# Position attention in a decoder of twelve sublayers: the row maxima enter the score product as rows of the stacks

## The reference

```
qh = q.reshape(B, 8, dq, Lq)          # q = x: B 64, 64 rows, Lq 256
kh = k.reshape(B, 8, dq, Lk)          # k = v = context, dq = 8
qk = einsum('bhdq,bhdl->bhql', qh, kh) / sqrt(dq)
ret = einsum('bhql,bhdl->bhdq', softmax(qk), vh)
x = layernorm(x + gamma * ret)
```

## Time and profile before

| | |
|---|---|
| median of three runs | 5089.75 us |
| profiled execution | 5091.97 us, span 5090.2 us |
| busy over the span | TensorE 89%, VectorE 65%, ScalarE 40%, POOL 30% |
| mean granted clock of TensorE | 0.961 |
| the fifth stage | about 864.7 to 1546.7 us of the span |
| one tile in it | about 19.2 us |

### The profile page before, as it was taken

One profiled execution on the slowest core, in us unless ns is written; L12 is line 12 of the kernel. 1 busy time (PEld: TensorE's weight loads), 2 busy tenths in 40 slices (PEclk: granted clock), 3 DMA queues, 4 the chain that ended last, 5 costly groups with the idle time before them and its releaser, 6 DMA issues.

```text
span 5090.2 us, 89514 instructions
## 1 busy us (share of the span) xinstructions
PE 4538.3 (89%) x33622; PEld 3195.2 (63%) x33669; DVE 3297.4 (65%) x6372; ACT 2040.4 (40%) x4326; POOL 1518.0 (30%) x3018
## 2 busy tenths in 40 slices
PE   8988997899997988888379999999997999999788
PEld 6766886566665667776246666666664666666455
DVE  5657236677776757878755555555554666666798
ACT  4544113354553433333135445455542434334222
POOL 1111005333321223333234344334432322222122
PEclk9999998899998999999589999999998999999999
DMA  1012000333320000000100000000001000000000
GB/s 42 2 51 61 1 6 31 79 78 75 77 57 32 1 8 8 7 8 7 67 30 1 1 1 1 1 1 1 1 1 56 9 7 9 8 8 6 5 14 16
DMA packets 114779, 111.54 MB, mean 22 GB/s; under 512 B 20848, under 2 KB 107056, under 8 KB 109872
## 3 DMA queue, kind: packets, MB, share of 16 engines
q1 hardware_dynamic: 114352, 105.82, 8.0%
HBM read 89.00 MB, written 16.78 MB: 21 GB/s over the span
## 4 chain that ended last, share of the span: by engine, by line
PE 50%; DVE 19%; issue 15%; POOL 9%; DMA 4%; ACT 3%; SPq 2%; POOLq 0%; DVEq 0%; ACTq 0%
PE banks L2246 13%; PE banks L2489 4%; PE banks L727 4%; POOL factors L2696 3%; PE banks L1761 3%; DMA stack<-parts_x 3%; PE banks L2312 2%; PE banks L1172 2%; PE banks L754 2%; DVE neg_max L1085 1%; PE banks L1671 1%; PE banks L2410 1%; POOL rstd L265 1%; PE banks L2338 1%; PE banks L499 1%
## 5 line engine op out<-in xcount | busy, mean ns | idle before, releaser
L263 POOL TENSOR_TENSOR var_eps<-mean_var,ln_eps 128x1 f32<-128x1 f32 x384 | 83.1, 216 | 1635.5 <-DVE mean_var L259 1091.3
L1085 DVE TENSOR_REDUCE neg_max<-banks 128x2 f32<-128x512 f32 x512 | 343.4, 682 | 191.4 <-PE banks L1075 184.8
L1202 ACT ACTIVATE exps<-banks 128x512 f32<-128x512 f32 x512 | 304.7, 597 | 309.1 <-PE banks L1156 292.3
L2300 DVE TENSOR_TENSOR q_normed<-banks,factors 128x512 f32<-128x512 f32 x256 | 176.4, 689 | 230.5 <-POOL factors L2290 230.5
L2267 ACT ACTIVATE squares<-banks 128x512 f32<-128x512 f32 x256 | 153.1, 598 | 411.6 <-PE banks L2246 411.6
L2290 POOL TENSOR_TENSOR factors<-mean_squares,minus_half 128x4 f32<-128x4 f32 x256 | 258.0, 1008 | 21.6 <-POOL mean_squares L2286 0.5
L2672 ACT ACTIVATE squares<-q_normed 128x512 f32<-128x512 f32 x160 | 100.8, 630 | 396.0 <-DVE q_normed L2662 396.0
L1075 PE MATMUL banks<-stack,stack 128*128 128x256 bf16 x1024 | 202.6, 281 | 63.3 <-DMA stack<-parts_x 57.7
L1761 PEld LDWEIGHTS banks<-yT,w_swiglu 128*128 128x128 f32 x2048 | 238.5, 193 | 30.2 <-issue 29.9
L1761 PE MATMUL banks<-yT,w_swiglu 128*128 128x128 f32 x2048 | 247.4, 277 | 8.5 <-DVE hidden L1785 8.5
L1155 PE MATMUL banks<-stack,stack 128*128 128x256 bf16 x1024 | 253.1, 274 | 1.6 <-ACT exps L1202 1.2
(11 more groups left out here) (381 smaller groups left out, 11140.0 us busy)
## 6 DMA issues: line engine op xcount, KB each, us to landing
contextT<-in_ctxT SPq DMA_DIRECT2D x96, 128.0 KB, 2.5
parts_context<-parts SPq DMA_DIRECT2D x96, 64.0 KB, 2.0
parts_x<-parts SPq DMA_DIRECT2D x96, 64.0 KB, 2.0
stack<-parts_context SPq DMA_DIRECT2D x32, 192.0 KB
stack<-parts_x SPq DMA_DIRECT2D x32, 192.0 KB
x_all<-in_x SPq DMA_DIRECT2D x1, 4096.0 KB, 14.1
context<-in_ctx SPq DMA_DIRECT2D x64, 64.0 KB, 2.2
context<-in_ctx SPq DMA_DIRECT2D x32, 128.0 KB, 2.3
```

The source lines that it names most:

```text
L1085: v.tensor_reduce(self.mx[s][:, :, g:g + 1], self.bM[g % 2].rearrange("p (h c) -> p h c", h=DH), AX.X, ALU.max, negate=True).then_inc(self ...
L1202: self.nc.scalar.activation(self.e[n % 8][:], self.bE[n % 2].rearrange("p (l c) -> p l c", l=DH), ACT.Exp, scale=self.TOK ** -0.5).then_in ...
```

## The change

It does these things:

- The rows 96 to 127 of the context stacks are set to one at the start, in POOL's setup (four memsets of bf16).
- SP moves the three parts of the turned maxima from `neg_maxT` into rows 96, 97 and 98 of the query stack (`move_max_sp`, three DMAs a tile, 8 KB each). The score matmul runs over all 128 rows and so takes the maxima off itself; the selector, its load and its 32 matmuls a tile are gone. The maximum pass runs over rows 0 to 95.
- In SP's program the moves (lag 4) stand behind the stacks (lag 2) and ahead of the parts (lag 1).
- Scores start at tick 10 of lag 4 (6 before). The first waits for the moves.
- The maximum pass has two pairs of banks, and a reduction takes two heads. The turned maxima go into the score banks, as one more use of them in turn (`slot`, `turn_slot`, `slot_free`).
- The weighing of four heads is issued in two halves, two ticks apart. `out_dve` takes the reciprocal in two halves and runs, as `tail_pool`, with lag 6 (5 before).

```diff
-    STEP, SCORES_FROM = 16, 6
+    STEP, SCORES_FROM, TURN_AT = 16, 10, 4
+    ROWS, MAX_ROWS = 96, 128
+    TURN_SLOT = STEP - SCORES_FROM + TURN_AT
-        self.bM, self.bN, self.bE, self.bO = (B[0], B[1]), B[2], (B[3], B[4]), (B[5], B[6])
+        self.bM, self.bE, self.bO = (p.ps[:, 0:2, :], p.ps[:, 2:4, :]), (B[4], B[5]), (B[6], B[7])
+        for n in range(self.STACK_BUFFERS):
+            last = pool.memset(self.kq[0][n][self.ROWS:self.MAX_ROWS], 1.0)
...
+            if g % 2 == 0:
+                if i >= 2:
+                    pe.wait_ge(self.maxed.sem, self.maxed.at(t, i - 1))
...
-                last = self.nc.tensor.matmul(self.bM[g % 2][:, h * D:(h + 1) * D], q[:, g, h * P:(h + 1) * P], k[:, g, :], start=True, stop=True)
+                last = self.nc.tensor.matmul(self.bM[i % 2][:, g % 2, h * D:(h + 1) * D], q[rows, g, h * P:(h + 1) * P], k[rows, g, :], start=True, stop=True)
...
+    def slot(self, t, n):
+        return (self.HEADS + 1) * t.index + n + (1 if n >= self.TURN_SLOT else 0)
+    def turn_slot(self, t):
+        return (self.HEADS + 1) * (t.index - 1) + self.TURN_SLOT
+    def slot_free(self, eng, slot):
+        t, n = divmod(slot - 2, self.HEADS + 1)
+        if slot < 2 or (n == self.TURN_SLOT and t + 1 >= self.NT):
+            return
+        if n == self.TURN_SLOT:
+            eng.wait_ge(self.m_copied.sem, self.m_copied.all(Tile(t + 1)))
+        else:
+            eng.wait_ge(self.exped.sem, self.exped.at(Tile(t), n + 1 - (1 if n > self.TURN_SLOT else 0)))
...
+    def move_max_sp(self, sp, t, s):
+        sp.wait_ge(self.m_copied.sem, self.m_copied.all(t))
+        for j in range(3):
+            sp.dma_start(self.stack(1, t)[self.ROWS + j:self.ROWS + j + 1, :, :],
+                         self.mT[s][32 * j:32 * j + self.HEADS, :]).then_inc(self.m_moved.sem(t), 16)
...
         if n == 0:
-            pe.wait_ge(self.m_copied.sem, self.m_copied.all(t))
+            pe.wait_ge(self.m_moved.sem(t), self.m_moved.all(t))
...
+        self.slot_free(pe, self.slot(t, n))
         for l in range(DH):
-            self.nc.tensor.matmul(out, k[:, h, l * P:(l + 1) * P], q[:, h, :], start=True, stop=False)
-            last = self.nc.tensor.matmul(out, self.sel[:, h, :], self.mT[s][:], start=False, stop=True)
+            last = self.nc.tensor.matmul(self.bE[self.slot(t, n) % 2][:, l * D:(l + 1) * D], k[rows, h, l * P:(l + 1) * P], q[rows, h, :], start=True, stop=True)
...
+    def weigh_at(self, pe, t, s, tick):
+        r, after = divmod(tick - self.SCORES_FROM - 5, 4)
+        if 0 <= r < 4 and after % 2 == 0:
+            self.weigh(pe, t, s, r, after // 2)
...
-            "pe": [[(5, self.score_late_pe), (4, self.score_pe), (4, self.turn_max_pe), (3, self.max_pe)]],
+            "pe": [[(6, self.weigh_last_pe), (5, self.score_late_pe), (4, self.score_from_pe), (4, self.turn_max_pe), (3, self.max_pe)]],
-            "dve": [[(4, self.split_max_dve), (5, self.out_dve), (3, self.max_dve)]],
-            "pool": [(3, self.values_pool), (5, self.tail_pool), (1, self.split_pool)],
-            "sp": [(2, self.stack_sp), (1, self.parts_sp), (0, self.source_sp)],
+            "dve": [[(4, self.split_max_dve), (6, self.out_dve), (3, self.max_dve)]],
+            "pool": [(3, self.values_pool), (6, self.tail_pool), (1, self.split_pool)],
+            "sp": [(2, self.stack_sp), (4, self.move_max_sp), (1, self.parts_sp), (0, self.source_sp)],
```

More of the change, by code:

```diff
@@ L968, in __init__ @@
         self.gamma = w("gamma", [P, 1]); self.load(self.gamma[:], p.ins["L1_xattn_gamma"])
-        self.sel = w("select", [P, self.HEADS, P], BF16); self.load(self.sel[:], p.ins["c_select"])
         self.ones = w("ones", [P, 4, 32]); self.load(self.ones[:], p.ins["c_den_columns"])
@@ L996, in __init__ @@
         self.v_ready = st("v_ready", 4)
-        self.made = st("made", 16)
-        self.maxed = st("maxed", 16)
+        self.made = st("made", 8)
+        self.maxed = st("maxed", 8)
         self.m_split = st("m_split", 5)
@@ L1001, in __init__ @@
         self.scored = st("scored", 16); self.exped = st("exped", 16); self.weighed = st("weighed", 4)
-        self.o_read = st("o_ready", 2)
-        self.zeroed = p.once("zeroed", 1)
+        self.o_read = st("o_ready", 3)
+        self.m_moved = p.transfers("m_moved", 3)
+        self.zeroed = p.once("zeroed", 3)
     def setup_pool(self, pool):
@@ L1007, in setup_pool @@
             for n in range(self.STACK_BUFFERS):
-                pool.memset(self.kq[i][n][:].bitcast(I32), 0)
+                last = pool.memset(self.kq[i][n][:].bitcast(I32), 0)
+        last.then_inc(self.zeroed.sem, 1)
+        pool.wait_ge(self.zeroed.sem, self.zeroed.at(1))
+        for n in range(self.STACK_BUFFERS):
+            last = pool.memset(self.kq[0][n][self.ROWS:self.MAX_ROWS], 1.0)
+        last.then_inc(self.zeroed.sem, 1)
+        pool.wait_ge(self.zeroed.sem, self.zeroed.at(2))
         for s in (0, 1):
@@ L1067, in max_pe @@
         k, q = self.stack(0, t), self.stack(1, t)
+        rows = slice(0, self.ROWS)
         pe.wait_ge(self.stacked.sem(t), self.stacked.all(t))
         for g in range(self.HEADS):
[L1070 to L1073, removed]
+            i = g // 2
+            if g % 2 == 0:
+                if i >= 2:
+                    pe.wait_ge(self.maxed.sem, self.maxed.at(t, i - 1))
+                elif begun(t - 1):
+                    pe.wait_ge(self.maxed.sem, self.maxed.at(t - 1, 8 + i - 1))
             for h in range(DH):
-                last = self.nc.tensor.matmul(self.bM[g % 2][:, h * D:(h + 1) * D], q[:, g, h * P:(h + 1) * P], k[:, g, :], start=True, stop=True)
-            last.then_inc(self.made.sem, 1)
+                last = self.nc.tensor.matmul(self.bM[i % 2][:, g % 2, h * D:(h + 1) * D], q[rows, g, h * P:(h + 1) * P], k[rows, g, :], start=True, stop=True)
+            if g % 2 == 1:
+                last.then_inc(self.made.sem, 1)
             yield
@@ L1080, in max_dve @@
         v = self.nc.vector
-        for g in range(self.HEADS):
-            dve.wait_ge(self.made.sem, self.made.at(t, g + 1))
-            if g == 0 and begun(t - 2):
+        for i in range(8):
+            yield
+            dve.wait_ge(self.made.sem, self.made.at(t, i + 1))
+            if i == 0 and begun(t - 2):
                 dve.wait_ge(self.m_split.sem, self.m_split.at(t - 2, 2))
-            v.tensor_reduce(self.mx[s][:, :, g:g + 1], self.bM[g % 2].rearrange("p (h c) -> p h c", h=DH), AX.X, ALU.max, negate=True).then_inc(self.maxed.sem, 1)
+            v.tensor_reduce(self.mx[s][:, :, 2 * i:2 * i + 2].rearrange("p h g -> p g h"), self.bM[i % 2].rearrange("p g (h c) -> p g h c", h=DH),
+                            AX.X, ALU.max, negate=True).then_inc(self.maxed.sem, 1)
             yield
@@ L1104, in split_max_dve @@
         v.tensor_copy(m3(2), self.m2[:]).then_inc(self.m_split.sem, 1)
+    def slot(self, t, n):
[10 more added lines that the diff above has]
+            eng.wait_ge(self.exped.sem, self.exped.at(Tile(t), n + 1 - (1 if n > self.TURN_SLOT else 0)))
     def turn_max_pe(self, pe, t, s):
-        for _ in range(4):
+        for _ in range(self.TURN_AT):
             yield
         pe.wait_ge(self.m_split.sem, self.m_split.all(t))
-        if begun(t - 1):
-            pe.wait_ge(self.m_copied.sem, self.m_copied.all(t - 1))
-        turned = self.bN[:].bitcast(BF16)
+        self.slot_free(pe, self.turn_slot(t))
+        turned = self.bE[self.turn_slot(t) % 2].bitcast(BF16)
         for h in range(DH):
@@ L1121, in copy_max_act @@
         if begun(t - 2):
-            act.wait_ge(self.scored.sem, self.scored.all(t - 2))
-        self.nc.scalar.copy(self.mT[s][:], self.bN[:].bitcast(BF16)[:, 0:D]).then_inc(self.m_copied.sem, 1)
+            act.wait_ge(self.m_moved.sem(t - 2), self.m_moved.all(t - 2))
+        self.nc.scalar.copy(self.mT[s][:], self.bE[self.turn_slot(t) % 2].bitcast(BF16)[:, 0:D]).then_inc(self.m_copied.sem, 1)
+    def move_max_sp(self, sp, t, s):
[3 more added lines that the diff above has]
+                         self.mT[s][32 * j:32 * j + self.HEADS, :]).then_inc(self.m_moved.sem(t), 16)
     def values_pool(self, pool, t, s):
@@ L1145, in score, with weigh @@
         if n == 0:
-            pe.wait_ge(self.m_copied.sem, self.m_copied.all(t))
+            pe.wait_ge(self.m_moved.sem(t), self.m_moved.all(t))
             if first(t):
                 pe.wait_ge(self.loaded.sem, self.loaded.done)
[L1149 to L1152, removed]
+        self.slot_free(pe, self.slot(t, n))
+        rows = slice(0, self.MAX_ROWS)
         for l in range(DH):
-            out = self.bE[n % 2][:, l * D:(l + 1) * D]
-            self.nc.tensor.matmul(out, k[:, h, l * P:(l + 1) * P], q[:, h, :], start=True, stop=False)
-            last = self.nc.tensor.matmul(out, self.sel[:, h, :], self.mT[s][:], start=False, stop=True)
```

(55 more changed lines are left out.)

## The result

The changed kernel takes 5415.98 us (median; 5412.72 to 5420.01) against 5088.07: a ratio of 1.0645, 95% interval 1.0626 to 1.0663, 328 us slower. The forecast was 5390, within 5280 to 5435. The profiled span is 5418.2 us.

The account below looks back on a forecast made before the run. TensorE and the POOL-SP-DMA chain were taken to bound a tile together at 19.1 us. The new one-step loop of 29.8 us over 27 steps, plus start and end, gave +300 us: 5390 us, range 5280 to 5435.

Parts of the forecast that it names:

- The bound before: In the old kernel, TensorE and the chain through POOL, SP and the DMAs both take 19.1 us a tile.
- The loop of one step: Score 0 waits at tick 10 for moves; their path through weighing, POOL, SP and DMAs closes each step: 29.8 us.
- POOL from the weighing to the parts: POOL's start, values, var_eps and rstd, then the split, after the weighing ends: 7.5 us a step.
- Parts: SP writes POOL's split parts to DRAM and waits for them: 3.3 us a step.
- Stacks and moves: From SP's issue of the stacks until the moves issued behind them land: 13.7 us a step.
- Moves landed to weighing done: TensorE from tick 10 to the half weighing of tick 13: 3.3 us at full clock, 5.3 with the lowered clock.
- Moves behind stacks: On SP's queue the moves wait for the stacks ahead and land 0.3 us behind contextT; called the dearest assumption.
- The rival with moves that pass: Moves don't wait behind the stacks on the queue: 21.2 us a step, +60 us, 5150 us; chance 0.12.
- The clock: Rival: TensorE's clock stays up through the wait or rises at once: 27.8 us a step, 5334 us; chance 0.14.
- TensorE's pace: Rival: maxima arrive ahead of tick 10, so TensorE sets the pace: 16.2 us a step, 5010 us; chance 0.04.
- The wait for the shared bank: On TensorE, score 11 waits for the copy behind one exponential, as maxima share score banks: some 0.8 us a step.
- the changes between bf16 and f32: On TensorE, four more switches of data type a step, 0.1 us each.

## Why the prediction was right

- **The bound before.** Two things ending together: shown by the split first in the kernel before (10 us) and by the run without moves (19.1 us a step for 19.4, with the selector's matmuls gone).
- **The loop of one step.** In the chain piece for piece. Its key was that POOL's split stands behind a wait for tick 13, and moving that one phase took 380 us away.
- **Its terms.** POOL from the weighing to the parts: 7.4 us (1210.18 to 1217.59) for 7.5. Parts: 3.26 for 3.3. Stacks and moves from 1220.85 to 1234.55: 13.7 for 13.7. Moves landed to weighing done: 6.1 us (1204.08 to 1210.18) for 5.3; this is the mis-sized term. I took the clock to rise 3.7 us after the return, as in the earlier trace rows; it rose after 5.4. The upper end of my range had 5.2, a bound that no row then showed. The step is 30.7 us for 29.8, and 27 x 0.9 = 24 us is nearly all of the 26 by which the 328 us exceed the 302 forecast (5088 to 5390). The start holds too: weighing done was forecast for 966.3, and POOL's copy behind it starts at 965.23. So the number is near because the terms are, and not by errors that cancel.
- **Moves behind stacks.** The last move landed 7.1 to 9.5 us after its issue, close to contextT's 8.7 to 10.7. By the Trainium skill's rule ("DMA: Bandwidth & Descriptors", section "Queues, rings and completion order") each DMA engine consumes its ring in order, so a move would wait on those engines that hold stack data and only there. The trace is in line with it and does not prove it: the count of the first two was full at 4.8 us, the last not before 8.7, and no row shows the engines one by one. ScalarE's own queue did not help while stacks were in flight (8.0 us), which is in line with the same page's "Issuing engines are not separate DMA queues".
- **The rival with moves that pass.** 21.2 us a step were forecast for it, 5150 us. Not reached by any run in the way it was written, since even another queue waits; moves first had 21.4 us a step, but by a loop of its own.
- **The clock.** The step with TensorE kept busy was 28.0 us, the rival said 27.8.
- **TensorE's pace.** Forecast 16.2 us a step and 5010 us; 17.0 and 5036 were measured once the loop was gone. The wait for the shared bank at tick 5 was sized well: the score matmul starts 0.8 us late. Too small were the changes between bf16 and f32: two ticks with half a weighing take 1.98 us and not 1.81, since half a weighing is 1.00 us for 0.93 and the matmuls behind it 0.32 for 0.22. Over eight such pairs that is 1.4 us where I had put 0.4.
- **Costs at the side.** The four memsets took 13.87 us (14), a reduction of 1024 elements 1.22 us (1.20); TensorE's first maxima started at 915.5 (917). A matmul over 96 rows took the same 273 ns at the median as one over 128.

## What to carry to other kernels

When a step is moved later in one engine's program, follow what waits for it through every other engine's program order until the path closes, and count in how many steps it closes: here one DMA issued behind another turned a loop of two steps into a loop of one. That the scores start four ticks later did not do it: the run without moves keeps that and has the loop of two steps. Moves with scores from tick 6 were not run. Look for the cheapest place to open it; it was not in the changed part, but in the order of three phases on POOL. A saving on the engine that is busy 98% of the time is worth nothing while a loop of the same length stands beside it.

## What the runs showed that I had not expected

- The same DMA bytes in smaller pieces landed in 4.6 to 9.0 us in place of 8.7 to 10.7 (contextT behind them), while in the tail of the large ones the mean share of the DMA engines was that of two to three busy ones in sixteen.
- TensorE's clock fell to 1.2 GHz near 1153.4, 2.9 us after a pause began that lasted only 1.7 us, with the engine busy again. Keeping it busy up to shortly before the wait did not keep the clock through this one. It is the only fall from 1050 to 1350, where the mean clock was 0.99 with the extra matmuls and 0.78 without.
- The first landing counts of three moves on one semaphore came at 4.8 us and the last at 8.7. No run shows which bytes were there at 4.8 us, so a wait for less than the full count has nothing to stand on.
